# A recommendation tower on one core: the upper layers run one step behind their operands

## The chip, the cores and the metric

The kernel runs on one core of a Trainium2 chip. What is measured is the device time of one execution in microseconds (us); a smaller number is better. The engines are TensorE (PE in the profile, PEld its weight loads), VectorE (DVE), ScalarE (ACT), GpSimd (POOL) and SyncE (SP). Each works through its own queue in order; semaphores order them against one another.

## What is computed

For 512 samples 26 rows of 64 numbers are gathered from embedding tables; each is projected to 128 numbers and normalised, 26 are mixed down to 32, normalised again, and together with a normalised dense row they give 33 vectors per sample. Their pairwise products go through a linear layer with a norm and then through three dense layers.

```
x = layer_norm(dense_t @ Wd.T, gd, bd)
y = layer_norm(jnp.einsum('bnd,ed->bne', sparse_t, Ws), gs, bs)
y = jnp.einsum('bne,pn->bep', y, Wsi)
y = layer_norm(y, gsi, bsi)
T = jnp.concatenate([x[:, None, :], jnp.swapaxes(y, 1, 2)], axis=1)
Z = jnp.einsum('bnd,bmd->bnm', T, T)
Zflat = Z[:, TRIL_I, TRIL_J]
out = layer_norm(Zflat @ Wl.T, gl, bl)[:, :384]
h = jnp.concatenate([out, r_dense_t], axis=1)
h = jnp.maximum(h @ W_top1 + b_top1, 0.0)
h = jnp.maximum(h @ W_top2 + b_top2, 0.0)
y = h @ W_top3
```

All of it is in float32, so each matmul stands in the profile as two passes (x6 is three matmuls).

## The kernel before

**Blocks, units, steps.** The 512 samples are four blocks (0 to 3, `LAST` is 3) of 128, each block four units of 32 samples, 16 units in all (`NU`). Units 0, 4, 8 and 12 have four pairs of gathered rows, the others three. One loop of steps n = 0 to 16 is written out on every engine, as a software pipeline: step n takes unit n through `transposes` (L311), the copy `rowsT` (ACT L557), `gram` (L318) and the variance of its rows (DVE L744 to L750); it takes unit n-1 through `mix` (L334), `vsb` (ACT L569), `embed` (L344), `biased` (DVE L768), `squares` (ACT L574), the sums `tss` (DVE L774), `deviations` (ACT L579) and `normalised` (DVE L781, L783, which writes T); and unit n-2 through `interact` (L357) and `interactions` (ACT L586, L588), which leaves the pairwise products in `zs`. Here "step n" begins, on TensorE, when it transposes unit n.

**Through DRAM and back.** SP writes each unit's `zs` to a scratch in DRAM (L269, L271), waits until that has landed and reads it back in the layout that the linear layer wants: `products` (three transfers into `zr`, L235) and `singles` (one into `zr4`, L241, two into `z9`, L244). For each block it does so twice, for units 0 to 2 of the block and then for unit 3. The first of these also waits until the linear layer of the block before is through (`u_done`), since `zr`, `zr4` and `z9` exist once. In the last block ACT issues the last unit's `singles`.

**Upper layers.** `upper` is the linear layer of a block in six matmuls of 128x512 (parts 0 to 3 from `zr`, 4 from `zr4`, 5 from `z9`). Then come `upper_norm` and `upper_scaled` (ACT), `turn` (L384), `hidden1_dense` and `hidden1` (L400, L414, L408), `hidden2` (L426) and `answer` (L434). For blocks 0 and 1 they stand in the step loop at fixed lags behind the block's first unit: upper [0, 1, 2] at U0, [3, 4, 5] at U1, turn and hidden1 at MLP, hidden2 at TOP, answer at ANS. In a step they stand behind `interact`. Nearly all of these share one PSUM bank, `pU`, and so `upper(k)` waits until ACT has copied the answer of block k-1 out (`o_sb`, L637); for block 0 the bank is that of the setup's small products. `x_row` (ACT L601) writes one row of `z9` per block.

**Setup inside the loop.** The linear layer's weights are made while the first units run: `weight_sums` and `weight_means`, `centred_weights` (ACT L649), `s_rows` (PE L454, DVE L807 to L810), `single_rows` (PE L461, L462, DVE L819, L820), `centred_rows` (ACT L655 to L659), `hidden_weights` (DVE L825) and `hidden_bias` (PE L470, DVE L830).

**Gathers.** POOL issues the 104 indirect DMAs of all units, two for each pair; every unit has its own place in SBUF, so POOL waits for nobody.

Of the kernel before, what the change touches and what calls it, by code (L numbers as in the profile page):

```python
# [21 lines left out]
NL = 5  # L22
# [36 lines left out]
def build(nc, tables, index, consts, small, ws_t, gs_row, wsi_rows, dense_t, wd_t, wl, wlx, w1, w2, out):  # L59
# [3 lines left out]
    with ExitStack() as ctx:  # L63
# [144 lines left out]
        block = ctx.enter_context(nc.Block())  # L208

        LAST = NBLK - 1  # L210
        U0, U1, MLP, TOP, ANS = UNITS + 2, UNITS + 3, UNITS + 4, UNITS + 5, UNITS + 6
        READS = 12

        def unit_rows(n):
# [10 lines left out]
        def tile_T(n):  # L225

            k, m = divmod(n, UNITS)
            return T[:, k % 2, :, US * m:US * (m + 1), :]

        def products(queue, k, units):  # L230

# [14 lines left out]
        @block.sync  # L246
        def _(sp):
            for dst, src, done in [(idx_in[:], index, ld_index), (ws_sb[:], ws_t, ld_ws), (const[:], consts, ld_const),
                                   (wsi_sb[:], wsi_rows, ld_wsi), (gs_sb[:], gs_row, ld_gs), (cols[:], small, ld_cols),
                                   (wd_sb[:], wd_t, ld_wd), (dense_sb[:], dense_t, ld_dense), (wlx_sb[:], wlx, ld_wlx)]:  # L250
                sp.dma_start(dst, src).then_inc(done, 16)
            for j in range(NL):
                if j % 2 == 0:

                    sp.wait_ge(r_done, 1 + j // 2)
                sp.dma_start(wl_sb[:, j, :], wl[:, j, :]).then_inc(ld_wl[j], 16)
            for c in range((USED + DENSE) // P):
                if c % 3 == 0:
                    sp.wait_ge(r_done, 4 + c // 3)
                first = P * c if P * c < USED else P * c + UO - USED  # L260
                sp.dma_start(w1_sb[:, c, :], w1[first:first + P, :]).then_inc(ld_w1, 16)
            sp.dma_start(w2_sb[:], w2.rearrange("(c p) n -> p c n", p=P)).then_inc(ld_w2, 16)
            for n in range(NU):
                k, m = divmod(n, UNITS)
                if m == 0 and k >= 2:

                    sp.wait_ge(zr_sb, 16 * READS * (k - 1))
                sp.wait_ge(zs_sb, n + 1)
                sp.dma_start(zscr[k % 2, :, m].rearrange("r p f -> p r f"),  # L269
                             zs[:, n % 2, 0:4 * QG * G8].rearrange("p (r f) -> p r f", r=4)).then_inc(zw[n % 2], 16)  # L270
                sp.dma_start(zscr9[k % 2, m], zs[:, n % 2, 4 * QG * G8:]).then_inc(zw[n % 2], 16)  # L271
                if m == UNITS - 2:
                    sp.wait_ge(zw[n % 2], 32 * (n // 2 + 1))
                    sp.wait_ge(zw[(n - 1) % 2], 32 * ((n - 1) // 2 + 1))
                    if k:
                        sp.wait_ge(u_done, k)
                    products(sp, k, range(0, UNITS - 1))
                    singles(sp, k, range(0, UNITS - 1))
                if m == UNITS - 1:
                    sp.wait_ge(zw[n % 2], 32 * (n // 2 + 1))  # L280
                    products(sp, k, range(m, UNITS))
                    if k < LAST:
                        singles(sp, k, range(m, UNITS))
            sp.wait_ge(o_sb, NBLK)
            sp.dma_start(out, ysb[:]).then_inc(out_done, 16)
            sp.wait_ge(out_done, 16)
# [14 lines left out]
        def _(pe):  # L301
# [59 lines left out]
            def upper(k, part):  # L361

                if part[0] == 0:
# [2 lines left out]
                    pe.wait_ge(zr_sb, 16 * READS * (k + 1))  # L366
                    pe.wait_ge(xrow_sb, k + 1)
                    if k == 0:
                        pe.wait_ge(w_ready, NL)
                        pe.wait_ge(w9c_ready, 1)  # L370
                for j in part:
# [118 lines left out]
            for n in range(NU + 1):  # L490
# [8 lines left out]
                if n == 0:  # L499
                    x_turned()  # L500
                if n == NU:
                    upper(LAST - 1, [4])
                if n:
                    embed(n - 1)
                if n == 0:
# [8 lines left out]
                    s_rows(range(0, 3))  # L514
                if n == 4:
                    s_rows(range(3, NL))
                    single_rows()
                if n == 5:
                    hidden_bias()
                if (k := block_at(n, TOP)) is not None:  # L520
                    hidden2(k)
# [4 lines left out]
                if (k := block_at(n, MLP)) is not None:  # L526
                    hidden1_dense(k)
                    hidden1(k)
                if n == NU - 2:
                    upper(LAST - 1, [0, 1, 2])  # L530
                if n == NU - 1:
                    upper(LAST - 1, [3])
                if n == NU:
                    upper(LAST - 1, [5])
            interact(NU - 1)
            hidden1_dense(LAST - 1)
            turn(LAST - 1)
# [11 lines left out]
        def _(act):  # L549
# [118 lines left out]
            for n in range(NU + 1):  # L668
# [29 lines left out]
                    interactions(n - 2)  # L698
                if n in (1, 2, 3):
                    weight_sums(range(2 * n - 2, min(2 * n, NL)))  # L700
                if n in (4, 5):
                    centred_weights(range(3 * n - 12, min(3 * n - 9, NL)))
                if n == 5:
                    centred_rows()
                if (k := block_at(n, U0)) is not None:
                    x_row(k)
                if n == NU - 2:
                    x_row(LAST - 1)
# [7 lines left out]
            x_row(LAST)  # L716
            upper_turned(LAST - 1)
            act.wait_ge(zw[(NU - 1) % 2], 32 * ((NU - 1) // 2 + 1))
            singles(act, LAST, range(UNITS - 1, UNITS))
            relu1(LAST - 1)  # L720
            upper_norm(LAST)
            upper_scaled(LAST)
# [8 lines left out]
        def _(dve):  # L731
# [147 lines left out]
            for n in range(NU + 1):  # L879
# [8 lines left out]
                if n:  # L888
                    variances(n - 1)
                    normalised(n - 1)  # L890
                if n == 3:
                    weight_means()
                if n == 4:
                    s_rows()
                    single_rows()
                if n == 5:
                    hidden_weights()
                    hidden_bias()
            upper_inverse(LAST - 1)
# [68 lines left out]
```

## Time and profile before

| | us |
|---|---|
| time, median of 3 runs | 204.39 (202.47 to 205.0) |
| the profiled execution, its own time | 204.47 |
| its span in the trace | 202.7 |
| TensorE busy | 155.0 (76%) |
| VectorE busy | 116.8 (58%) |
| ScalarE busy | 85.2 (42%) |
| GpSimd busy | 102.9 (51%) |
| mean granted TensorE clock | 0.899 of full |

Busy times are sums over the span. Times in the rows below are counted from the span's start. A row of the timeline gives start, duration, engine, line, operation, tiles, count, and in brackets how long the engine was idle before it and what ended that.

### The profile page before, as it was taken

How to read it: one execution, taken by the hardware profiler on the slowest of the kernel's cores; microseconds unless marked ns; L12 is line 12 of the kernel's file. 1: busy time of each engine (PE TensorE's matmuls, PEld its weight loads, DVE VectorE, ACT ScalarE, POOL GpSimd, SP SyncE). 2: the span in 40 equal slices, each digit the busy share in tenths (PEclk: the TensorE clock that was granted, in tenths of full speed). 3: DMA queues.
4: the chain of work that ended last, by engine and by line, in shares of the span. 5: the costliest groups of instructions: out<-in, count | busy, mean ns of one | idle time of the engine just before them, and what ended most of it. 6: DMA issues, size and time to landing. Idle time of an engine off the chain costs nothing.

```text
span 202.7 us, 4648 instructions
## 1 busy us (share of the span) xinstructions
PE 155.0 (76%) x1865; PEld 106.3 (52%) x1865; DVE 116.8 (58%) x279; ACT 85.2 (42%) x229; POOL 102.9 (51%) x108
## 2 busy tenths in 40 slices
PE   0547787597806995599699939987995999496996
PEld 0435354463302683266497725657883464395684
DVE  2896239876828259819754990779099358600000
ACT  2002317735351193527526650546476034712063
POOL 3787777777777777777787777771000000000000
PEclk9995569889985699799999997999999699889999
DMA  5514132151935122312135241121411101152000
GB/s 143 173 27 129 32 124 81 25 186 37 269 67 76 28 58 37 57 26 55 28 73 65 52 69 26 29 55 44 53 32 18 31 0 31 32 63 36 0 3 0
DMA packets 38521, 12.01 MB, mean 59 GB/s; under 512 B 34114, under 2 KB 35266, under 8 KB 38499
## 3 DMA queue, kind: packets, MB, share of 16 engines
q1 hardware_dynamic: 34354, 8.26, 18.8%
q0 software_dynamic: 3328, 3.41, 8.3%
q8 instruction: 15, 0.25, 0.5%
q10 hardware_dynamic: 816, 0.02, 0.2%
q14 instruction: 8, 0.06, 0.1%
HBM read 9.46 MB, written 2.23 MB: 58 GB/s over the span
## 4 chain that ended last, share of the span: by engine, by line
PE 35%; POOL 16%; DMA 12%; DVE 11%; issue 9%; ACT 8%; SPq 7%; ACTq 0%; DVEq 0%
POOL rows L295 16%; PE pU L373 7%; DMA zscr<-zs 7%; PE pV L334 6%; PE pA L318 4%; SPq L235 3%; PE pU L414 3%; DVE t L768 2%; DVE evar L747 2%; DVE prod L744 2%; PE pU L400 2%; PE pA L373 2%; DMA z<-zscr 2%; PE pA L311 2%; ACT t L574 2%
## 5 line engine op out<-in xcount | busy, mean ns | idle before, releaser
L295 POOL DMA_INDIRECT rows<-in_tables,idx x104 | 102.7, 988 | 34.3 <-issue 31.4
L744 DVE TENSOR_TENSOR prod<-pA,rows 128x384 f32<-128x384 f32 (+1 forms) x16 | 9.4, 590 | 42.7 <-PE pA L318 42.6
L373 PE MATMUL pU<-wg,zr 128*128 128x512 f32 x24 | 17.4, 865 | 9.6 <-DMA z<-zscr 6.1
L334 PE MATMUL pV<-wexp,srow 128*64 128x192 f32 (+4 forms) x256 | 23.6, 335 | 0.7 <-DVE srow L759 0.7
L783 DVE TENSOR_TENSOR T<-t,trs 128x512 f32<-128x512 f32 x32 | 22.2, 694 | 1.1
L574 ACT ACTIVATE t<-t 128x512 f32<-128x512 f32 x32 | 19.5, 629 | 5.8 <-DVE t L768 5.7
L334 PEld LDWEIGHTS pV<-wexp,srow 128*64 128x64 f32 x256 | 17.7, 156 | 6.5 <-issue 2.7
L557 ACT COPY rowsT<-pA 128x384 f32<-128x384 f32 (+1 forms) x16 | 7.9, 497 | 31.0 <-PE pA L311 30.9
L318 PE MATMUL pA<-gbd,rowsT 128*128 128x128 f32 x104 | 18.7, 327 | 2.9 <-ACT rowsT L557 2.7
L768 DVE TENSOR_TENSOR t<-pT,bias 128x512 f32<-128x512 f32 x32 | 20.5, 683 | 0.4 <-PE pT L344 0.4
L774 DVE TENSOR_REDUCE tss<-t 128x16 f32<-128x512 f32 x32 | 20.4, 677 | 0.1
L357 PEld LDWEIGHTS pZ<-T 128*32 128x32 f32 x1024 | 11.9, 112 | 12.8 <-issue 6.4
L318 PEld LDWEIGHTS pA<-gbd,rowsT 128*128 128x128 f32 x104 | 15.4, 224 | 6.1 <-ACT rowsT L557 4.5
L344 PE MATMUL pT<-vsb,wscg 64*128 64x512 f32 x64 | 18.3, 648 | 0.0
L357 PE MATMUL pZ<-T 128*32 128x34 f32 x1024 | 14.1, 202 | 2.9 <-DVE T L783 2.9
L311 PE MATMUL pA<-const,rows 128*128 128x128 f32 x52 | 9.8, 307 | 8.3 <-DMA rows<-in_tables,idx 8.3
L311 PEld LDWEIGHTS pA<-const,rows 128*128 128x128 f32 x52 | 6.9, 158 | 16.4 <-issue 13.7
L373 PEld LDWEIGHTS pU<-wg,zr 128*128 128x128 f32 x24 | 7.2, 324 | 15.5 <-issue 15.3
L563 ACT ACTIVATE esd<-evar,eps 128x6 f32<-128x6 f32 (+1 forms) x16 | 4.8, 299 | 23.0 <-DVE evar L750 16.8
L569 ACT COPY vsb<-pV 128x512 f32<-128x512 f32 x16 | 9.3, 584 | 8.8 <-PE pV L334 8.5
L781 DVE RECIPROCAL trs<-tsd 128x16 f32<-128x16 f32 x32 | 7.9, 246 | 7.0 <-ACT tsd L579 6.9
L579 ACT ACTIVATE tsd<-tss,eps 128x16 f32<-128x16 f32 x32 | 9.4, 305 | 3.9 <-DVE tss L774 3.6
(153 smaller groups left out, 203.2 us busy)
## 6 DMA issues: line engine op xcount, KB each, us to landing
zscr<-zs SPq DMA_DIRECT2D x16, 128.0 KB, 2.0
rows<-in_tables,idx POOLq DMA_INDIRECT x104, 2.5
wl_sb<-in_wl SPq DMA_DIRECT2D x5, 256.0 KB, 2.7
w_sb<-in_w SPq DMA_DIRECT2D x5, 256.0 KB
dense_sb<-in_dense_t SPq DMA_DIRECT2D x1, 512.0 KB, 4.6
w_sb<-in_w SPq DMA_DIRECT2D x1, 512.0 KB, 6.3
zr<-zscr SPq DMA_DIRECT2D x4, 96.0 KB
zr<-zscr SPq DMA_DIRECT2D x4, 72.0 KB
```

The lines of the kernel that those rows point to most:

```text
L295: pool.indirect_dma_start(out=rows[:, j, h * D:(h + 1) * D], out_offset=None, in_=tables, in_offset=bass.IndirectOffsetOnAxis(ap=idx[:, 2 ...
L311: got = nc.tensor.transpose(pA[n % 2][:, P * j:P * (j + 1)], rows[:, first + j, :], ident)
L318: got = mm(pA[n % 2][:, P * j:P * (j + 1)], rowsT[:, n % 2, j, :], gbd[:], start=True, stop=True)
L334: got = mm(pV[(n - m + u) % 2][D * h:D * (h + 1), PJ * (a - US * u):PJ * (z + 1 - US * u)], srow[:, n % 2, i, D * h:D * (h + 1)], wexp[:, ...
L344: mm(pT[h][:], wscg[D * h:D * (h + 1), :], vsb[D * h:D * (h + 1), n % 2, :], start=True, stop=True).then_inc(y_done, 1)
L357: got = mm(pZ[PJ * s:PJ * (s + 1), NCOL * g:NCOL * (g + 1)], t[:, h, i, 0:PJ], t[:, h, i, :], start=True, stop=True)
L373: mm(upper_bank(k)[:], zr[:].rearrange("p a (g j) -> p (a g) j", j=4)[:, :, j], wg[:, j, :], start=j == 0, stop=False)
L574: a.activation(t2[:, h], t1[:, n % 2, h], ACT.Square).then_inc(t_sq, 1)
L744: v.tensor_tensor(prod[:, 0:count, :], pA[n % 2][:, 0:P * count].rearrange("p (j r) -> p j r", r=P), rows[:, first:first + count, :], ALU. ...
L768: v.tensor_tensor(t1[:, n % 2, h], pT[h][:].rearrange("p (a b) -> p a b", b=PJ), bias[:].unsqueeze(1).to_broadcast([P, US, PJ]), ALU.add). ...
L774: v.tensor_reduce(out=tss[:, h], in_=t2[:, h], op=ALU.add, axis=AX.X).then_inc(t_var, 1)
L783: v.tensor_tensor(tile_T(n)[:, h, :, 0:PJ], t1[:, n % 2, h], trs[:, h].unsqueeze(2).to_broadcast([P, US, PJ]), ALU.mult).then_inc(t_sb, 1)
```

## The change

- The lags U0, U1, MLP, TOP and ANS grow by one step each; `x_row` of blocks 0 and 1 stays in the step it was in.
- In the setup `single_rows` moves from step 4 to 5 and `hidden_bias` with `hidden_weights` from 5 to 6; on ACT `centred_weights` moves from steps 4 and 5 to 5 and 6 and `centred_rows` from 5 to 6; on DVE `weight_means` moves from step 3 to 4. `upper(0)` gets a wait for `b1_ready`.
- The linear layer of block 2 stood as [0, 1, 2] in step 14, [3] in step 15, [4] and [5] in step 16. It now stands as [0, 1] in step 15, and [2] and [3, 4, 5] in step 16.
- In block 3 the products are read back for units 0 and 1 and then for 2 and 3 (before: 0 to 2 and then 3).

```diff
-        U0, U1, MLP, TOP, ANS = UNITS + 2, UNITS + 3, UNITS + 4, UNITS + 5, UNITS + 6
+        U0, U1, MLP, TOP, ANS = UNITS + 3, UNITS + 4, UNITS + 5, UNITS + 6, UNITS + 7
...
+        def ahead(k):
+
+            return UNITS - 2 if k == LAST else UNITS - 1
...
-                if m == UNITS - 2:
+                if m == ahead(k) - 1:
                     sp.wait_ge(zw[n % 2], 32 * (n // 2 + 1))
                     sp.wait_ge(zw[(n - 1) % 2], 32 * ((n - 1) // 2 + 1))
                     if k:
                         sp.wait_ge(u_done, k)
-                    products(sp, k, range(0, UNITS - 1))
-                    singles(sp, k, range(0, UNITS - 1))
+                    products(sp, k, range(0, m + 1))
+                    singles(sp, k, range(0, m + 1))
                 if m == UNITS - 1:
                     sp.wait_ge(zw[n % 2], 32 * (n // 2 + 1))
-                    products(sp, k, range(m, UNITS))
+                    sp.wait_ge(zw[(n - 1) % 2], 32 * ((n - 1) // 2 + 1))
+                    products(sp, k, range(ahead(k), UNITS))
...
                     if k == 0:
+                        pe.wait_ge(b1_ready, 1)
...
                 if n == NU:
-                    upper(LAST - 1, [4])
+                    upper(LAST - 1, [2])
...
                 if n == 4:
                     s_rows(range(3, NL))
+                if n == 5:
                     single_rows()
-                if n == 5:
+                if n == 6:
                     hidden_bias()
...
-                if n == NU - 2:
-                    upper(LAST - 1, [0, 1, 2])
                 if n == NU - 1:
-                    upper(LAST - 1, [3])
+                    upper(LAST - 1, [0, 1])
                 if n == NU:
-                    upper(LAST - 1, [5])
+                    upper(LAST - 1, [3, 4, 5])
...
-                if n in (4, 5):
-                    centred_weights(range(3 * n - 12, min(3 * n - 9, NL)))
-                if n == 5:
+                if n in (5, 6):
+                    centred_weights(range(3 * n - 15, min(3 * n - 12, NL)))
+                if n == 6:
                     centred_rows()
-                if (k := block_at(n, U0)) is not None:
+                if (k := block_at(n, U0 - 1)) is not None:
                     x_row(k)
...
             act.wait_ge(zw[(NU - 1) % 2], 32 * ((NU - 1) // 2 + 1))
-            singles(act, LAST, range(UNITS - 1, UNITS))
+            act.wait_ge(zw[NU % 2], 32 * ((NU - 2) // 2 + 1))
+            singles(act, LAST, range(ahead(LAST), UNITS))
...
-                if n == 3:
+                if n == 4:
                     weight_means()
-                if n == 4:
                     s_rows()
+                if n == 5:
                     single_rows()
-                if n == 5:
+                if n == 6:
                     hidden_weights()
                     hidden_bias()
```

On TensorE, from the end of step 4, the order before was (L454 is `s_rows`, L461 and L462 `single_rows`, L311 the transposes that open step 5):

```order
L357 MATMUL pZ<-T 32x34 x32
L454 MATMUL pU<-wl_sb,beye 32x512 x2
L461 MATMUL pU<-wlx_sb,cols 1x512
L462 MATMUL pU<-wbraw,bp 1x512
L311 MATMUL pA<-const,rows 128x128 x3
L334 MATMUL pV<-wexp,srow 64x160 x2
```

In the changed kernel (its line numbers are up to six higher: L316 the transposes, L323 `gram`, L349 `embed`, L467 and L468 `single_rows`) the same place reads:

```order
L460 MATMUL pU<-wl_sb,beye 32x512 x2
L316 MATMUL pA<-const,rows 128x128 x3
L339 MATMUL pV<-wexp,srow 64x160 x2
L339 MATMUL pV<-wexp,srow 64x192 x4
L339 MATMUL pV<-wexp,srow 64x64 x2
L339 MATMUL pV<-wexp,srow 64x128 x2
L323 MATMUL pA<-gbd,rowsT 128x128 x3
L349 MATMUL pT<-vsb,wscg 128x512 x2
L362 MATMUL pZ<-T 32x34 x32
L467 MATMUL pU<-wlx_sb,cols 1x512
L468 MATMUL pU<-wbraw,bp 1x512
```

The single-row products now stand behind the whole of step 5's pipeline work.

On TensorE at the end, before, from the last part of step 14 on (L373, L376, L378 are the parts of `upper(2)`, the last row is `interact(15)`; the second L334 is `mix(15)`):

```order
L373 MATMUL pU<-wg,zr 128x512
L334 MATMUL pV<-wexp,srow 64x192 x4
L334 MATMUL pV<-wexp,srow 64x160 x2
L376 MATMUL pU<-wg,zr 128x512
L344 MATMUL pT<-vsb,wscg 128x512 x2
L357 MATMUL pZ<-T 32x34 x32
L378 MATMUL pU<-w9c,z 128x512
L357 MATMUL pZ<-T 32x34 x32
L400 MATMUL pT<-dense_sb,w_sb 128x128 x8
```

And in the changed kernel, from the end of step 15 on (L379, L382, L384 are the same parts):

```order
L379 MATMUL pU<-wg,zr 128x512 x2
L339 MATMUL pV<-wexp,srow 64x192 x4
L339 MATMUL pV<-wexp,srow 64x160 x2
L379 MATMUL pU<-wg,zr 128x512
L349 MATMUL pT<-vsb,wscg 128x512 x2
L362 MATMUL pZ<-T 32x34 x32
L379 MATMUL pU<-wg,zr 128x512
L382 MATMUL pU<-wg,zr 128x512
L384 MATMUL pU<-w9c,z 128x512
L362 MATMUL pZ<-T 32x34 x32
L406 MATMUL pT<-dense_sb,w_sb 128x128 x8
```

Three parts instead of one stand between the last two `interact`, and three instead of five ahead of the last `embed`.

On SP's queue the end of the loop was, before (each pair of L269 and L271 writes one unit; the first pair here is unit 14's):

```order
L269 DMA zscr<-zs 128x4x64
L271 DMA zscr<-zs 128x16
L235 DMA zr<-zscr 64x12x32
L235 DMA zr<-zscr 48x12x32
L235 DMA zr<-zscr 16x12x32
L241 DMA zr<-zscr 128x12x8
L244 DMA z<-zscr 32x12x8 x2
L269 DMA zscr<-zs 128x4x64
L271 DMA zscr<-zs 128x16
L235 DMA zr<-zscr 64x4x32
```

And now (from behind unit 13's write on):

```order
L239 DMA zr<-zscr 64x8x32
L239 DMA zr<-zscr 48x8x32
L239 DMA zr<-zscr 16x8x32
L245 DMA zr<-zscr 128x8x8
L248 DMA z<-zscr 32x8x8 x2
L273 DMA zscr<-zs 128x4x64
L275 DMA zscr<-zs 128x16
L273 DMA zscr<-zs 128x4x64
L275 DMA zscr<-zs 128x16
L239 DMA zr<-zscr 64x8x32
```

The writes of units 14 and 15 both stand behind the first read of the block, and so behind its wait for `u_done`.

## Rows read from the trace of the kernel before

**Rows 1.** The page: the chain that ended last, shares of the span by engine
```profile
PE 35%; POOL 16%; DMA 12%; DVE 11%; issue 9%; ACT 8%; SPq 7%; ACTq 0%; DVEq 0%
```
**Rows 2.** The waits: who waited for whom, us in total, times, longest
```profile
PE pU L373 <- DMA z<-zscr: 6.1, 2, 3.3
```
**Rows 3.** The gathers' line: ns min/median/max, first and last start, and their landing
```profile
L295 POOL DMA_INDIRECT rows<-in_tables,idx x104: 940/945/1575, 3.3 to 136.5; - x104
...
DMA to landing us min/median/max: 2.3/2.5/5.4
```
**Rows 4.** The timeline where steps 4 and 5 meet
```profile
57.05 0.32 ACT L586 COPY zs<-pZ 128x192 f32<-128x192 f32 x1 [2.27 <-DMA zscr<-zs]
...
57.38 2.23 ACT L649 ACTIVATE wg<-wl_sb,gg 128x512 f32<-128x512 f32 x3
...
59.51 0.49 ACT L579 ACTIVATE tsd<-tss,eps 128x16 f32<-128x16 f32 x2
...
62.57 1.01 PE L461 MATMUL pU<-wlx_sb,cols 32*1 32x512 f32 x1 [7.81 <-DVE wbraw L807]
...
63.21 0.47 DVE L810 TENSOR_SCALAR w<-wlx_sb,cols 32x512 f32<-32x512 f32 x1
```
**Rows 5.** The timeline of steps 5 to 8: DVE, ACT and PE
```profile
69.54 0.56 DVE L744 TENSOR_TENSOR prod<-pA,rows 128x384 f32<-128x384 f32 x1 [3.66 <-PE pA L318]
...
72.66 0.30 ACT L586 COPY zs<-pZ 128x192 f32<-128x192 f32 x1
...
76.00 0.49 ACT L579 ACTIVATE tsd<-tss,eps 128x16 f32<-128x16 f32 x2
...
78.14 1.27 DVE L825 TENSOR_SCALAR w1g<-w_sb,cols 128x512 f32<-128x512 f32 x3
...
83.42 4.42 PE L373 MATMUL pU<-wg,zr 128*128 128x512 f32 x6 [3.57 <-ACT z L601]
...
94.66 0.60 PE L311 MATMUL pA<-const,rows 128*128 128x128 f32 x4
```
**Rows 6.** The timeline of steps 10 to 14: PE, and ACT's copy of an answer
```profile
112.70 0.49 PE L311 MATMUL pA<-const,rows 128*128 128x128 f32 x3
...
118.34 0.24 ACT L637 COPY ysb<-pU 1x128 f32<-1x128 f32 x1
...
120.64 4.59 PE L373 MATMUL pU<-wg,zr 128*128 128x512 f32 x6 [3.28 <-DMA z<-zscr]
...
132.22 0.60 PE L311 MATMUL pA<-const,rows 128*128 128x128 f32 x4
...
143.69 0.49 PE L311 MATMUL pA<-const,rows 128*128 128x128 f32 x3
...
150.02 0.49 PE L311 MATMUL pA<-const,rows 128*128 128x128 f32 x3
```
**Rows 7.** Windows: stretch, its us, busy of each engine, PEclk, DMA share, GB/s
```profile
120.60:125.10 4.50, 4.46 (x7) 2.02 (x8) 0.98 (x3) 0.00 (x0) 3.41 (x4) 0.62 0.28 54
125.10:132.20 7.10, 7.10 (x100) 4.47 (x99) 4.49 (x10) 3.46 (x9) 5.45 (x6) 1.00 0.13 30
```
**Rows 8.** The timeline of the end: PE and SP's queue
```profile
167.85 1.14 PE L334 MATMUL pV<-wexp,srow 128*64 128x192 f32 x12 [0.40 <-DVE srow L759]
...
169.98 1.13 PE L344 MATMUL pT<-vsb,wscg 64*128 64x512 f32 x4
...
175.73 1.13 PE L357 MATMUL pZ<-T 128*32 128x34 f32 x64 [2.87 <-DVE T L783]
...
176.83 2.40 SPq L235 DMA_DIRECT2D zr<-zscr  x3
...
181.54 0.50 SPq L271 DMA_DIRECT2D zscr<-zs  x1
...
183.44 1.72 SPq L235 DMA_DIRECT2D zr<-zscr  x3
...
186.60 3.82 PE L373 MATMUL pA<-wg,zr 128*128 128x512 f32 x8 [2.01 <-DMA zr<-zscr]
```

More of the change, by code:

```diff
@@ L276, in _ @@
                         sp.wait_ge(u_done, k)
-                    products(sp, k, range(0, UNITS - 1))
-                    singles(sp, k, range(0, UNITS - 1))
+                    products(sp, k, range(0, m + 1))
+                    singles(sp, k, range(0, m + 1))
                 if m == UNITS - 1:
                     sp.wait_ge(zw[n % 2], 32 * (n // 2 + 1))
-                    products(sp, k, range(m, UNITS))
+                    sp.wait_ge(zw[(n - 1) % 2], 32 * ((n - 1) // 2 + 1))
+                    products(sp, k, range(ahead(k), UNITS))
                     if k < LAST:
-                        singles(sp, k, range(m, UNITS))
+                        singles(sp, k, range(ahead(k), UNITS))
             sp.wait_ge(o_sb, NBLK)
```

## The prediction, made before the changed kernel had run

> **What bounds the kernel now.** I read the chain of work that ended last first. TensorE has 35% of it, GpSimd only 16%, and DMA, DVE and "issue" share a third [rows 1]: no engine alone is the bound, so the question is where TensorE stands still. Then the gathers, since they feed everything: POOL issues its 104 from buffers of their own; the first starts at 3.3 us, the last at 136.5 [rows 3], one per 133.2 / 103 = 1.29 us, and the last lands at about 139. But step 15, which needs it, starts only at about 162: step 14 starts at 150.02 and is like step 10, which lasts from 112.70 to 125.1, 12.4 with its waits [rows 6, 7]. The gathers are 23 us ahead by then: from step 5 on the kernel is held by TensorE and what TensorE waits for. The timeline shows four long waits there: 7.81 us at 62.57 for the DVE copy of `s_rows` [rows 4], 3.57 us ahead of `upper(0)` for ACT's `x_row` [rows 5], 3.28 us ahead of `upper(1)` [rows 6] and the other wait for the same transfer ahead of `upper(2)`, 6.1 - 3.3 = 2.8 us [rows 2]. After the last three TensorE also runs slow: the window with `upper(1)` has a granted clock of 0.62, most of it at 1.2 GHz, the next one 1.00 [rows 7]. Three parts take 4.5 us there, where in the tail four take 3.82 us [rows 8], so 2.75 us for three is the price at full clock, 1.7 us less each time.
>
> **What holds the setup.** ACT gets `zs` of unit 2 off its hands only at 57.05, after waiting for unit 0's scratch write; then three `wg` (2.23 us) stand ahead of `tsd` at 59.51, which DVE needs for T and then for `s_rows`, through at 63.21 + 0.47 = 63.7 [rows 4]. TensorE sits at `single_rows` behind that.
>
> **The change, step by step.** I walk the start of each step, in the trace's own time. Steps 0 to 4 don't change, nor does the write that lands at 57.
>
> *Steps 5 to 7.* `zs` ends at 57.6 and `tsd` follows at once, 1.9 us earlier, so DVE is through `s_rows` at 61.8. The gathers of unit 5 (40 of them, 3.3 + 39 x 1.29 and 2.5 to land, so about 56.2) let TensorE start step 5 at once instead of waiting for `single_rows`; its `gram` waits for ACT's `rowsT` until 58.7 and is done well before 61.8. So `prod` of unit 5 starts at 61.8, now 69.54 [rows 5]. From here DVE and ACT hold the loop, by distances of rows 5 and 4. `prod` to `zs`: 72.66 - 69.54 = 3.1, so 64.9. `zs` to `tsd` with three `wg`: 59.51 - 57.05 = 2.5, so 67.4. `tsd` to the end of T: 78.14 - 76.00, 2.2 with its pipelining, so 69.6; then the two one-row copies of `single_rows`, 1.4 for two DVE instructions of 512 (estimated from `prod`, 0.56 for 384), so `prod` of unit 6 at 71.0. Step 6 again: `zs` 74.1; `tsd` behind two `wg`, `centred_rows` (76.00 - 72.66 = 3.3) and now `x_row` (0.3) at 77.75; T through at 79.95; `w1g` 1.27 and `b1p` 0.15: 81.4. Here is what the change gives back: setup work that TensorE no longer waits for still stands ahead of `rowsT` and T on ACT and DVE. `gram(7)` can start at 78.7; with `embed` and `interact` (one each at 0.9, 1.0, 0.7) TensorE reaches `upper(0)` at 81.5, where the new wait for `b1_ready` ends too, and [0, 1, 2] takes 2.75. **Step 8 starts at 84.3 at full clock.** TensorE will have stood 2 us or more ahead of `gram(7)`; with the slow clock that followed the waits of 3.57 and 3.28 us it would be up to 1.7 later. I take 85.0. Now it is 94.66, with parts [3, 4, 5] done, which cost 2.6.
>
> The Trainium skill, TensorE: Matmul & The Clock Gate, section "What's actually happening", says that the throttled state is the default and activity releases it; the window rows agree (0.62, then 1.00). By it the long wait that is left, ahead of `gram(7)`, would be followed by slow matmuls and step 8 would start near 86; by the full clock at 84.3.
>
> *Steps 8 to 15.* Each kind of step has a row at full clock. A step with [3, 4, 5]: 7.1 [rows 7], with a fourth pair 0.35 more, 7.45. A step with turn and hidden1: 143.69 - 132.22 = 11.5, its waits of some 1.8 for ACT in it. A step with hidden2: 150.02 - 143.69 = 6.3 [rows 6]. The step with [0, 1, 2] was 12.4 (112.70 to 125.1, the next step's start). There the transfer is a step old now, but the answer of the block before is copied out in the same step as before, and that is what is late next: ACT's copy ends at 118.34 + 0.24, so 5.9 us after the step's start [rows 6]. `upper` starts at 5.95 instead of 7.95, waits 1.3 instead of 3.3 and keeps its clock: 5.95 + 2.75 = 8.7. `mix` of these steps needs `srow` from DVE, whose loop is about 6.2 long, under each of them. Starts: step 9 at 92.45, 10 at 103.95, 11 at 110.25, 12 at 118.95, 13 at 126.4, 14 at 137.9, 15 at 144.2. In step 15 only two parts: 5.95 + 1.85, so `mix(15)` at **152.0**, now 167.85. The gathers stay ahead, by about 3 us at steps 9, 12 and 13 (their last lands at 115.7 for step 12) and 5 at step 15.
>
> *The end.* From `mix(15)` to `embed(15)` stands one part as before, 169.98 - 167.85 = 2.1: 154.1. From there to `interact(15)` is a chain over DVE and ACT, 175.73 - 169.98 = 5.75, with 2.87 of waiting in it [rows 8]; the two parts more that stand there now (1.7) fit into it. So 159.85. The linear layer of block 2 is through at 154.1 + 1.8 + 2.75 = 158.7. SP then issues six reads, 4.15 us (176.83 until the first of unit 15's two writes, 0.5 ahead of 181.54), until 162.9; then two writes of each of two units at 0.5, the last issued at 164.4, landed 1.9 later (183.44 - 181.54) at 166.3; then the last products, as before 186.60 - 183.44 = 3.15 after that: `upper(3)` at **169.45**, 9.6 after `interact(15)`, now 10.9. Behind 186.60 nothing changes: 202.7 - 186.6 = 16.1. Span 185.55, and 1.8 around it (204.47 - 202.7): 187.3; the profiled execution stands at the median, so that needs no correction. Sum by places: 5.7 in the setup with its slow clock, 7.4 in blocks 1 and 2 (two waits cut by 2.0 and 1.5, two slow stretches of 1.7, the rest rounding), 1.8 from two parts moved behind the last `embed`, 1.3 in the last read-back; 17 us with rounding.
>
> The new waits, bounded: `b1_ready` costs nothing to 1 us, as DVE and TensorE arrive together. SP's wait for `u_done` now holds the writes of units 14 and 15. Their cover is the chain to `interact(15)`: `zs` of unit 15 comes 1.7 after 159.85, at 161.6, and SP is free for it at 163.9 (now the data come 1.7 after 175.73, at 177.4, and the write is issued at 181.0). If `u_done` came 1 us later, the end would.
>
> **Rivals.**
> *A, forecast, 184 to 191.5:* above. Chance 0.74, and 0.02 for still less.
> *B, the setup keeps more.* ACT's and DVE's serial work in steps 5 to 7 is the only stretch for which no row shows the new order. If each of three loops costs 1.5 to 2.5 us more than the distances taken (a slow TensorE, a late landing: gathers took up to 5.4 [rows 3]), step 8 starts at 90 to 92: 192 to 199. Against it: DVE and ACT distances don't depend on TensorE's clock. 0.15.
> *C, waits come back elsewhere.* The step with [0, 1, 2] keeps its 12.4 and the slow clock, because some operand is still late: 3.7 us in each of two blocks, and B on top: 200 to 208. Against it: both transfers are issued a whole step before. 0.06.
> *D, slower: the gathers stretch.* In the changed kernel DVE works the same hours in fewer. If a gather waited while DVE runs, its pace would rise. It begins to cost when the pace passes 1.32 us (steps 9, 12, 13) and the kernel is slower by 2% when the last gather lands at 166, a pace of 1.55. For: the longest gather is 1575 ns. Against: median 945 and minimum 940 under a DVE that is busy 58% of the time [rows 3]. 0.03; a small stretch of 0.05 us only moves A to about 190.
> The Trainium skill, SBUF - State Buffer, names this mechanism: an exclusive lock on a port pair that VectorE shares with GpSimd, through which descriptors are written ("the DVE blocks DMA trap"). By that rule D would be likely; the trace does not show it, since the gathers' median lies 5 ns above their minimum.
>
> **The numbers.** Predicted 187.3. From 184 (full clock everywhere, 1 us less in the last read-back, early step 8) to 196 (most of B). A measurement here tells a difference of about 2%, 4 us. Faster takes A, B and the rare faster case: 0.91; the same C: 0.06; slower D: 0.03.
>
> **What would show it.** The wait at `single_rows` is gone; the first `prod` after it starts near 62; the longest TensorE wait is the one ahead of `gram(7)`; `upper(1)` and `upper(2)` start about 6 us into their steps with a granted clock of 1.00; between the last two `interact` TensorE waits under 2 us; the last read-back is issued within 7 us of `interact(15)`. Wrong would be: step 8 later than 88, a wait of 3 us ahead of `upper(1)`, transposes that wait for gathers after step 6 by more than a us, gathers at more than 1.35 us.

## The result

The changed kernel takes 193.58 us in the median (192.1 to 195.37), the kernel before in the same session 204.69 (202.47 to 206.72); the ratio is 0.947, with a 95% interval of 0.934 to 0.960. Timed twice more it gave 192.31 and 192.33 us, at ratios of 0.948 and 0.944. So the change makes the kernel 5.2 to 5.6% faster, some 11 us. Forecast were 187.3 us, or 17 us, with a range of 184 to 196. Executions of one kernel spread by 1 to 4%, and one of the kernel with ACT's order changed took 240.97 us at a mean granted clock of 0.603; medians given here are of all executions, ratios of the faster ones alone.

The profiled execution took 192.1 us, with a span of 190.3. First the page: busy times hardly moved (155.0 to 153.4 us on TensorE, 116.8 to 117.2 on DVE), and the chain that ended last now has more of TensorE and of the gathers in it, and less than half of the DMA (5% instead of 12%) [rows 1].

```profile
PE 153.4 (81%) x1865; PEld 106.1 (56%) x1865; DVE 117.2 (62%) x279; ACT 84.4 (44%) x229; POOL 103.1 (54%) x108
...
PE 40%; POOL 20%; DVE 12%; issue 10%; ACT 7%; DMA 5%; SPq 4%; ACTq 0%
```

The place where steps 4 and 5 meet, in the timeline of the changed kernel (start, duration, engine, line, and in brackets the idle time and its end), which answers to [rows 4]:

```profile
56.77 0.32 ACT L591 COPY zs<-pZ 128x192 f32<-128x192 f32 x1 [1.76 <-DMA zscr<-zs]
...
57.10 0.52 ACT L584 ACTIVATE tsd<-tss,eps 128x16 f32<-128x16 f32 x2
...
57.82 0.70 PE L316 MATMUL pA<-const,rows 128*128 128x128 f32 x3 [2.66 <-DMA rows<-in_tables,idx]
...
60.90 0.48 DVE L816 TENSOR_SCALAR w<-wlx_sb,cols 32x512 f32<-32x512 f32 x1
...
62.22 0.56 DVE L750 TENSOR_TENSOR prod<-pA,rows 128x384 f32<-128x384 f32 x1 [0.84 <-PE pA L323]
...
64.00 0.59 PE L467 MATMUL pU<-wlx_sb,cols 32*1 32x512 f32 x1
```

TensorE no longer stands 7.81 us at the single rows: it reaches them at 64.00 without a wait and has done step 5 ahead of them. `tsd` follows `zs` at once, `s_rows` are through at 61.4 (63.7 before), and `prod` of unit 5 starts at 62.22 instead of 69.54.

Steps 6 to 8, which answer to [rows 5]:

```profile
68.69 0.94 PE L323 MATMUL pA<-gbd,rowsT 128*128 128x128 f32 x6 [1.98 <-ACT rowsT L562]
...
71.62 2.81 PE L476 MATMUL pU<-cols,w_sb 128*128 128x1 f32 x24
...
74.79 1.95 PE L339 MATMUL pV<-wexp,srow 128*64 128x192 f32 x16
...
79.33 1.65 PE L323 MATMUL pA<-gbd,rowsT 128*128 128x128 f32 x6 [2.59 <-ACT rowsT L562]
...
80.91 2.08 PE L349 MATMUL pT<-vsb,wscg 64*128 64x512 f32 x4
...
84.03 3.48 PE L379 MATMUL pU<-wg,zr 128*128 128x512 f32 x6
...
87.34 0.60 PE L316 MATMUL pA<-const,rows 128*128 128x128 f32 x4
```

Here are the waits that took over: two for ACT's `rowsT`, 1.98 and 2.59 us. Around the second lies a slow stretch (`gram` 1.65 us, 0.94 at full clock). It doesn't begin with the wait: `mix(6)`, ahead of it, takes 1.95 us already, where `mix(5)` took 1.20, and the window that ends as `gram(7)` starts has a granted clock of 0.58:

```profile
74.30:79.30 5.00, 2.44 (x21) 1.79 (x20) 2.15 (x5) 4.89 (x14) 4.07 (x4) 0.58 0.29 57
```

(columns: us, busy of PE, PEld, DVE, ACT, POOL, granted clock, DMA share, GB/s). By windows of 1 us the clock is 1.00 until 75 and 0.50 from 76 to 85. What stands ahead of its fall is `hidden_bias` (L476), 24 passes of one column each. Step 8 starts at 87.34, 94.66 before.

Blocks 1 and 2, which answer to [rows 6]:

```profile
112.35 0.49 PE L316 MATMUL pA<-const,rows 128*128 128x128 f32 x3
...
118.28 2.96 PE L379 MATMUL pU<-wg,zr 128*128 128x512 f32 x6 [1.04 <-ACT ysb L642]
...
128.38 0.49 PE L316 MATMUL pA<-const,rows 128*128 128x128 f32 x3
...
139.61 0.49 PE L316 MATMUL pA<-const,rows 128*128 128x128 f32 x3
...
145.67 0.49 PE L316 MATMUL pA<-const,rows 128*128 128x128 f32 x3
```

`upper(1)` comes 5.9 us into its step, waits 1.04 us for the copy of the answer instead of 3.28 for the transfer, and its three parts take 2.8 us instead of 4.4, with a granted clock of 1.00.

And the end, which answers to [rows 8]: TensorE first, then SP's queue.

```profile
156.00 1.13 PE L349 MATMUL pT<-vsb,wscg 64*128 64x512 f32 x4
...
161.74 0.77 PE L362 MATMUL pZ<-T 128*32 128x34 f32 x64 [1.03 <-DVE T L789]
...
172.52 5.52 PE L379 MATMUL pA<-wg,zr 128*128 128x512 f32 x8 [3.23 <-DMA zr<-zscr]
```
```profile
163.09 2.08 SPq L248 DMA_DIRECT2D z<-zscr  x2
...
166.74 0.51 SPq L275 DMA_DIRECT2D zscr<-zs  x1
...
168.50 1.76 SPq L239 DMA_DIRECT2D zr<-zscr  x3
```

`interact(15)` starts at 161.74, 14.0 us earlier than before. But from there to the end of the span it is 28.6 us, before 202.7 - 175.73 = 27.0. The end got longer by 1.6 us where 1.3 less was forecast: the wait ahead of `upper(3)` grew from 2.01 to 3.23 us, and its first four parts from 3.7 to 5.4 us to the next part's start. From `interact(15)` to `upper(3)` it is 10.8 us, as good as before (10.9); the wait is longer because TensorE has its own work ahead of it done in 7.5 us instead of 8.9. Before, that work had begun at the lower clock, behind the 2.87 us ahead of `interact(15)` (`hidden1_dense` 3.00 us, now 2.05).

### The profile page after: what moved, and what is told of

It is laid out like the page before. It is cut to its first block, busy times and chain, and to the rows that moved or that the text cites. A ratio compares the mean times of both kernels' runs of the same rounds, so it can differ in the third digit from the quotient of the medians.

```text
span 190.3 us, 4653 instructions
## 1 busy us (share of the span) xinstructions
PE 153.4 (81%) x1865; PEld 106.1 (56%) x1865; DVE 117.2 (62%) x279; ACT 84.4 (44%) x229; POOL 103.1 (54%) x108
## 3 DMA queue, kind: packets, MB, share of 16 engines
q0 software_dynamic: 3328, 3.41, 10.8%
## 4 chain that ended last, share of the span: by engine, by line
PE 40%; POOL 20%; DVE 12%; issue 10%; ACT 7%; DMA 5%; SPq 4%; ACTq 0%
POOL rows L300 20%; PE pU L379 6%; PE pV L339 6%; PE pA L323 5%; PE pT L349 3%; PE pA L379 3%; PE pU L420 3%; PE pZ L362 2%; DVE t L774 2%; PE pU L406 2%; DVE evar L753 2%; DVE prod L750 2%; DMA rows<-in_tables,idx 2%; PE pA L316 2%; SPq L239 2%
## 5 line engine op out<-in xcount | busy, mean ns | idle before, releaser
L339 PE MATMUL pV<-wexp,srow 128*64 128x192 f32 (+4 forms) x256 | 24.3, 343 | 0.2 <-DVE srow L765 0.2
L323 PE MATMUL pA<-gbd,rowsT 128*128 128x128 f32 x104 | 18.6, 326 | 6.6 <-ACT rowsT L562 6.4
L339 PEld LDWEIGHTS pV<-wexp,srow 128*64 128x64 f32 x256 | 18.2, 160 | 6.3 <-issue 3.1
L323 PEld LDWEIGHTS pA<-gbd,rowsT 128*128 128x128 f32 x104 | 15.3, 222 | 9.7 <-ACT rowsT L562 7.9
L349 PE MATMUL pT<-vsb,wscg 64*128 64x512 f32 x64 | 19.8, 699 | 0.0
L362 PEld LDWEIGHTS pZ<-T 128*32 128x32 f32 x1024 | 12.2, 112 | 12.4 <-issue 8.5
L316 PE MATMUL pA<-const,rows 128*128 128x128 f32 x52 | 9.5, 300 | 10.1 <-DMA rows<-in_tables,idx 10.1
L316 PEld LDWEIGHTS pA<-const,rows 128*128 128x128 f32 x52 | 6.4, 152 | 17.5 <-issue 15.0
L362 PE MATMUL pZ<-T 128*32 128x34 f32 x1024 | 14.6, 203 | 1.1 <-DVE T L789 1.0
L379 PE MATMUL pU<-wg,zr 128*128 128x512 f32 x24 | 13.5, 681 | 2.3 <-ACT ysb L642 2.3
L794 DVE RECIPROCAL urs<-usd 128x1 f32<-128x1 f32 x4 | 0.8, 192 | 19.0 <-ACT usd L612 18.9
```

The costliest lines, as they stand in the source:

```text
L316: got = nc.tensor.transpose(pA[n % 2][:, P * j:P * (j + 1)], rows[:, first + j, :], ident)
L323: got = mm(pA[n % 2][:, P * j:P * (j + 1)], rowsT[:, n % 2, j, :], gbd[:], start=True, stop=True)
L339: got = mm(pV[(n - m + u) % 2][D * h:D * (h + 1), PJ * (a - US * u):PJ * (z + 1 - US * u)], srow[:, n % 2, i, D * h:D * (h + 1)], wexp[:, ...
L349: mm(pT[h][:], wscg[D * h:D * (h + 1), :], vsb[D * h:D * (h + 1), n % 2, :], start=True, stop=True).then_inc(y_done, 1)
L362: got = mm(pZ[PJ * s:PJ * (s + 1), NCOL * g:NCOL * (g + 1)], t[:, h, i, 0:PJ], t[:, h, i, :], start=True, stop=True)
L379: mm(upper_bank(k)[:], zr[:].rearrange("p a (g j) -> p (a g) j", j=4)[:, :, j], wg[:, j, :], start=j == 0, stop=False)
```

## The experiments

Each kernel was timed against the kernel before on the same chip, in three sessions. The changed kernel itself was timed in the first (with the kernels up to "The setup undone") and in the third (with the matmuls in step 7), but not in the second. For the four kernels of the second session the difference to the changed kernel is given both between medians and between ratios to the kernel before, and neither is sure to 1 us.

**The changed kernel again.**

> The changed kernel again, beside its variants. Expected 192 to 194 us, with the two things that the prediction undersized: steps 6 to 8 slow (step 8 at about 87) and a wait of about 3 us ahead of upper(3), after which it runs slow.

192.31 us, ratio 0.948 (0.937 to 0.958). Its trace differs from the first in one place that matters. The windows from 79.0 to 84.6 us of the first trace and of this one:

```profile
79.00:84.60 5.60, 5.27 (x75) 3.44 (x76) 5.43 (x14) 1.85 (x5) 4.21 (x5) 0.50 0.14 24
```
```profile
79.00:84.60 5.60, 5.47 (x80) 3.73 (x81) 5.46 (x14) 1.90 (x5) 4.08 (x6) 0.96 0.12 23
```

From `gram(7)` on, the first trace runs at 1.2 GHz (0.50) into `upper(0)`, the second nearly all at 2.4. In the second TensorE had been slow earlier, in most of step 6 (66 to 72) and again in the first part of step 7 (76 to 79), where DVE and ACT cover it, and so it waited only 0.27 us ahead of `gram(7)`. It reached `upper(0)` at 81.90, just as `b1p` was there (81.52 + 0.15), and step 8 started at **84.67**: the forecast's 84.3 at full clock. In the first, `b1p` was there at 81.87 and `upper(0)` started at 84.03 all the same. `gram(7)` starts within 0.2 us of the same time in both (79.33 and 79.13), and from there to step 8 it is 8.0 us in the first and 5.5 in the second. So the same kernel has 2.7 us of play at step 8, by where the slow stretch falls. At the end both traces show the same: a wait of 3.23 and 3.61 us ahead of `upper(3)`, which takes 5.52 us.

**The last block's split undone.**

> The changed kernel with the last block read back as before (units 0 to 2, then 3). Theory S, the split carries a part of the gain (my sum gave the read-back 1.3 us): slower than the changed kernel by 1.3 us or more. Theory N, the smaller last read gives back what the earlier write gains: unit 14's data at 159.6, landed at 163, six reads of 4.15, unit 15's writes landed at 169.6, upper(3) at 172.7 against 172.5: same within 0.5 us, and still a wait of some 3 us ahead of upper(3).

```diff
         def ahead(k):
 
-            return UNITS - 2 if k == LAST else UNITS - 1
+            return UNITS - 1
```

192.25 us against 192.31: same. Theory N holds. TensorE and SP's queue at the end of this kernel:

```profile
159.75 0.77 PE L362 MATMUL pZ<-T 128*32 128x34 f32 x64 [1.03 <-DVE T L789]
...
170.83 2.04 PE L379 MATMUL pA<-wg,zr 128*128 128x512 f32 x3 [3.54 <-DMA zr<-zscr]
```
```profile
160.64 2.39 SPq L239 DMA_DIRECT2D zr<-zscr  x3
...
165.34 0.50 SPq L275 DMA_DIRECT2D zscr<-zs  x1
...
167.32 1.72 SPq L239 DMA_DIRECT2D zr<-zscr  x3
```

`upper(3)` comes 11.1 us after `interact(15)`; in the changed kernel 10.8 in the first trace and 170.57 - 159.41 = 11.2 in the second. The reads of units 0 to 2 start at 160.64 here, of units 0 and 1 at 160.80 in the changed kernel: both stand just behind the end of `upper(2)`, and SP's time for six reads follows. The smaller last read is quicker (170.83 - 167.32 = 3.5 us from its issue to `upper(3)`, against 172.52 - 168.50 = 4.0), the later write eats that up. This part of the change is worth nothing that can be measured here.

**The setup alone.**

> The kernel before with the setup moved one step (single rows in 5, hidden bias, hidden weights and centred rows in 6) and the lags as they were. Theory C, the two halves need each other: the wait at the single rows goes, but upper(0) then stands in step 6 behind b1p, which DVE has at about 82: a wait of 7 us there, step 7 at about 86 instead of 87.8, 1 to 2 us gained in all (203). Theory I, the parts add up: 5 us or more gained (under 200).

```diff
                 if n == 4:
                     s_rows(range(3, NL))
+                if n == 5:
                     single_rows()
-                if n == 5:
+                if n == 6:
                     hidden_bias()
```

(with the same moves on ACT and DVE as in the change, and the wait for `b1_ready`). 204.62 us (202.67 to 207.18), where the kernel before had 206.48 over its wide spread of 202.11 to 209.71. The shortest executions of the two differ by 0.6 us, so no gain is shown; theory I, 5 us or more, is out. Its trace shows why:

```profile
81.92 4.31 PE L374 MATMUL pU<-wg,zr 128*128 128x512 f32 x6 [7.74 <-DVE b1p L832]
```

The 7.81 us that stood at the single rows stand in step 6 instead, 7.74 us for `b1p`, with the slow clock at their end still (4.31 us for three parts). Step 7 starts at 86.07, 87.68 before, which is theory C's 86. The wait has moved, as the setup's chain on DVE and ACT was not made shorter.

**The setup undone.**

> The changed kernel with the setup where it was before, so lags, block 2 in three pieces and the last block's split alone. The 7.8 us wait at the single rows stays, the waits ahead of upper(1) and upper(2) shrink to about 1.2 us at full clock. Theory C: step 8 at about 90 instead of 87.3, 3 us slower than the changed kernel (196), so this half carries three quarters of the gain. Theory I, the setup is worth its 7.8 us: slower than the changed kernel by 6 us or more (199).

```diff
                 if n == 4:
                     s_rows(range(3, NL))
+                    single_rows()
                 if n == 5:
-                    single_rows()
-                if n == 6:
                     hidden_bias()
```

(and likewise on ACT and DVE). 196.08 us, 3.8 slower than the changed kernel; ratio 0.964 (0.953 to 0.975). That is nearer to theory C (3 us) than to the 6 us or more of theory I. So the lags and the pieces of block 2 carry 3.6% by themselves, some two thirds of the gain; the setup adds 1.6% to them, and alone no gain is shown. The lags and the pieces of block 2 were not taken apart, so the 1.8 us that the forecast gave to the pieces were not tested. In the trace of this kernel the wait at the single rows is there (6.24 us) and the waits ahead of `upper(1)` and `upper(2)` are 1.25 and 1.28 us, near the changed kernel's 1.04 and 1.28. Step 8 starts at 92.35 there, not at about 90: ahead of it stand a wait of 2.57 us for DVE's `srow` and a slow `mix(6)` (2.18 us). That execution, 198.09 us, was the longest of the four.

**ACT's order in the setup.**

> The changed kernel with ACT's weight work taken out of the place ahead of tsd and rowsT: three wg in step 6 and two wg with the centred rows in step 7, behind vsb, where ACT stands idle 3.4 to 3.8 us. Theory A, ACT's order in steps 5 and 6 gives back the setup gain: the waits of 1.98 and 2.59 us ahead of gram(6) and gram(7) go, TensorE keeps its clock, step 8 starts at 82 to 83.5 (then held by its gathers) instead of 87.3, total 4 to 5 us less. Rival G, the gathers or DVE hold these steps: under 2 us less.

```diff
+                if n in (6, 7):
+                    centred_weights(range(3 * n - 18, min(3 * n - 15, NL)))
+                if n == 7:
+                    centred_rows()
                 if n < NU:
                     row_deviation(n)
...
-                if n in (5, 6):
-                    centred_weights(range(3 * n - 15, min(3 * n - 12, NL)))
-                if n == 6:
-                    centred_rows()
```

188.99 us, ratio 0.925 (0.913 to 0.937), against 0.948 and 0.944 for the changed kernel: 3.3 us less by medians, 3.8 to 4.6 by ratios. ACT and TensorE in its steps 6 to 8:

```profile
73.43 0.30 ACT L591 COPY zs<-pZ 128x192 f32<-128x192 f32 x1
...
74.28 0.31 ACT L584 ACTIVATE tsd<-tss,eps 128x16 f32<-128x16 f32 x1
...
74.99 0.46 ACT L562 COPY rowsT<-pA 128x384 f32<-128x384 f32 x1
...
75.50 1.65 PE L323 MATMUL pA<-gbd,rowsT 128*128 128x128 f32 x6 [0.50 <-ACT rowsT L562]
...
77.69 0.15 DVE L836 TENSOR_TENSOR b1p<-pU,cols 128x4 f32<-128x4 f32 x1
```
```profile
91.15 0.52 PE L316 MATMUL pA<-const,rows 128*128 128x128 f32 x3 [0.33 <-DMA rows<-in_tables,idx]
```

`tsd` comes 0.9 us after `zs` instead of 3.8 (74.62 to 78.41 in the changed kernel), the waits for `rowsT` fall to 0.70 and 0.50, and `b1p` is there at 77.7 instead of 81.9. Step 8 starts at 83.40. Theory A holds in its main part: ACT's serial weight work ahead of `tsd` and `rowsT` was what gave the setup gain back. One part of it fails. TensorE does not keep its clock: with only 0.50 us of waiting ahead of `gram(7)`, the granted clock is 0.50 from 75 to 81 all the same, and `gram(7)` takes 1.65 us, `embed` 2.08 and `upper(0)` 3.42. So the slow stretch of step 7 does not come from the wait ahead of `gram(7)`. The next limit shows too, transposes that wait for their gathers in steps 9, 12 and 13 (0.33, 0.40, 0.24 us).

**Matmuls in the wait ahead of `upper(3)`.**

> The changed kernel with three matmuls of 128x512 whose result nobody reads, put where TensorE waits 3.2 us ahead of upper(3). They take 2.6 us and fit. Theory W, the wait costs twice, by itself and by the lower clock behind it: upper(3) takes 3.7 instead of 5.4 us for its first four parts and the total falls by 1.5 to 1.7 us. Rival: upper(3) is slow for another reason (its operands just landed): no change.

```diff
             hidden1(LAST - 1)
+            for _ in range(3):
+                mm(pA[1][:], ident, w1_sb[:, 0, :], start=True, stop=True)
             upper(LAST, range(0, NL + 1))
```

190.83 us, ratio 0.935 (0.920 to 0.950), 1.5 us below the changed kernel by medians, 1.8 to 2.6 by ratios; intervals overlap, so the trace decides:

```profile
161.20 0.77 PE L362 MATMUL pZ<-T 128*32 128x34 f32 x64 [1.03 <-DVE T L791]
...
168.58 2.74 PE L546 MATMUL pA<-w_sb,const 128*128 128x512 f32 x6
171.41 3.82 PE L379 MATMUL pA<-wg,zr 128*128 128x512 f32 x8
```

With the wait filled, the same four parts take 3.82 us instead of 5.52, and from `interact(15)` to the end of the span it is 187.5 - 161.2 = 26.3 us instead of 28.6. The wait ahead of `upper(3)` cost twice: 1.7 us of its price is the lower clock behind it. The granted clock from 171.4 to 175.1 is 1.00, in the changed kernel it is 0.68 from 172.5 to 177.9; so the rival, that the operands had only just landed, is out. The kernel before says the same: there `upper(3)` starts as its operands land and takes 3.82 us too.

**The read-back buffers twice.**

> The changed kernel with zr, zr4 and z9 twice, so that the reads of a block wait for the linear layer two blocks back only. In block 3 SP then reads units 0 and 1 early and has the writes of units 14 and 15 out as soon as their data are there. Theory Q, SP's queue held by u_done sets the end: unit 15 landed at about 166 instead of 168.5, upper(3) at 169.3 to 170 and at full clock, total 4 to 5 us less. Rival: the landing time of the last read sets it: under 2 us less.

```diff
-        zr = sb("zr", [P, 4 * UNITS, G8 * 4])
+        zr = sb("zr", [P, 2, 4 * UNITS, G8 * 4])
...
-                    if k:
-                        sp.wait_ge(u_done, k)
+                    if k > 1:
+                        sp.wait_ge(u_done, k - 1)
```

(`zr4` and `z9` likewise, each use indexed by k % 2, and `x_row` waiting one block further back.) 187.53 us, ratio 0.913 (0.900 to 0.926): 6 to 7 us below the changed kernel by ratios, 4.8 by medians across sessions. SP's queue and TensorE:

```profile
154.50 1.76 SPq L239 DMA_DIRECT2D zr<-zscr  x3
...
163.75 1.33 SPq L275 DMA_DIRECT2D zscr<-zs  x1
...
166.17 1.76 SPq L239 DMA_DIRECT2D zr<-zscr  x3
```
```profile
170.20 2.11 PE L379 MATMUL pA<-wg,zr 128*128 128x512 f32 x4 [0.67 <-DMA zr<-zscr]
```

The reads of units 0 and 1 are issued at 154.5, while `mix(15)` runs, and the last unit's write no longer stands behind them: 8.2 us from `interact(15)` (161.99) to `upper(3)` instead of 10.8, and a wait of 0.67 us that leaves the clock alone. To the end of the span 24.3 us, 4.3 less. Theory Q holds. The gain by medians, 4.8 us, is about what the trace shows. The rest of the gain by ratios, 2 to 3 us, is not explained; it may be the spread of the kernel before (7.7 us in that session), but that is not shown.

**Both together.**

> Both: ACT's order and the second set of read-back buffers. If the two theories hold and don't share a cause, the gains add up to 8 to 10 us below the changed kernel, 183 to 185, unless the gathers bind (the last lands at 139 and step 15 would start at about 141).

184.36 us (183.86 to 185.01), ratio 0.904 (0.894 to 0.913): the fastest of the kernels here, 8 us below the changed one by medians (3.3 and 4.8 us were the two gains alone), so the two gains add up. Its span is 182.4. Nothing waits ahead of `gram(7)` any more, and still the granted clock is 0.50 from 72 to 78, from `hidden_bias` (3.56 us) on. Step 8 starts at 82.40, and steps 9 and 12 wait 0.43 and 0.61 us for gathers. Its gathers:

```profile
L300 POOL DMA_INDIRECT rows<-in_tables,idx x104: 940/944/1581, 3.4 to 136.9; - x104
```

The pace of the gathers is that of [rows 3], with DVE busy 64% of the span instead of 58%.

**Matmuls in the wait of step 7.**

> The changed kernel with three matmuls of 128x512 whose result nobody reads in step 7, behind mix, where TensorE waits 2.6 us for ACT's rowsT ahead of gram(7). Theory W, what made steps 7 and 8 later than forecast is the lower clock that follows this wait: gram(7) at 0.94 instead of 1.65 us, embed 1.1 instead of 2.1, upper(0) 2.9 instead of 3.5, step 8 starts at 84.3 to 85.5 instead of 87.3, and the time falls by up to 2 us. Rival V, DVE and ACT hold step 7 (b1p at 81.9) and the clock there is covered: step 8 no earlier than 86.5.

```diff
+                if n == 7:
+                    pe.wait_ge(t1_sb, 12)
+                    for _ in range(3):
+                        mm(pT[0][:], ident, w1_sb[:, 0, :], start=True, stop=True)
                 if n < NU:
                     gram(n)
```

> The changed kernel once more, on the same chip as the run with extra matmuls in step 7: 192 to 194 us; its trace shows how much steps 6 to 8 move from execution to execution (step 8 at 87.34 in the first trace, 84.67 in the second).

192.50 us, against 192.33 for the changed kernel in the same session (ratios 0.947 and 0.944): no gain. Theory W is not borne out: step 8 starts at 89.35, not at 84.3 to 85.5. In the trace with the extra matmuls TensorE ran at 1.2 GHz in `gram(6)` and `embed(6)` (71 to 75) and again from `hidden_bias` on (78 to 81), so that it came to the extra matmuls only at 81.35. ACT's `rowsT` was there at 81.50, so there was no wait left to fill, and the extra matmuls held `gram(7)` back until 84.03. It took 0.83 us and `upper(0)` 2.94, at full clock, but later than without them. A filler helps only where the wait is sure to be.

The third trace of the changed kernel, timed beside this one, has step 8 at 88.27, later than either of the first two. Its slow stretch, too, begins at 76, ahead of the wait of 2.63 us for `rowsT`. Taken together, ten traces have `hidden_bias` in this place. In nine of them the clock falls while it runs or within 1.3 us of its end, whatever wait follows (none to 7.7 us). In the tenth, that with matmuls ahead of `upper(3)`, it falls only behind the wait ahead of `gram(7)` (3.32 us). In the kernel before, `hidden_bias` stood behind a stretch that was slow until 69.7, and the clock stayed full behind it. No run moved or widened `hidden_bias`, so what makes the clock fall there is open.

## Why the prediction was right, and where not

**What bounds, right.** TensorE and what it waits for was the bound; behind step 6 the gathers hold a step only when ACT's order is changed too, and then by 0.61 us at most. The rival that the gathers stretch under a busier DVE (D) fell: 947 ns in the median in the changed kernel, 945 before, 944 in the kernel with both improvements. The Trainium skill, SBUF — State Buffer, section "Who interferes with whom", says that `tensor_tensor` has no two-port mode, and `tensor_reduce` none on this chip; it is in such a mode that VectorE blocks a transfer of GpSimd's. These two kinds are over four fifths of DVE's busy time here, so "by that rule D would be likely" was too strong, and the gathers' times agree with that.

**Steps 5 to 7, right in their chain.** Forecast and seen: `prod` of unit 5 at 61.8 and 62.22, of unit 6 at 71.0 and 71.50, `tsd` of step 6 at 77.75 and 78.41, `b1p` at 81.4 and 81.87. That the setup gives most of its gain back on ACT and DVE was in the forecast; the kernel with the setup alone and the one with ACT's order changed show it. Step 5 started at 57.82 instead of 56.2, since its gathers took 3.6 to 5.0 us to land and not 2.5; DVE waited 0.84 us for `gram(5)` by it.

**Step 8, mis-sized.** 85.0 was forecast, seen 87.34, and 84.67 in the second trace. The term is the slow clock from `gram(7)` on, for which I took 0.7 us of a bound of 1.7. From `gram(7)` to step 8 the first trace takes 2.5 us more than the second; `gram(7)` itself came 0.6 later than forecast. The bound was drawn too low: the slow stretch takes `gram` (+0.7), `embed` (+1.0), `interact` (+0.4) and part of `upper(0)` (+0.5), not `upper(0)` alone. And the reason given was not the right one: I had the stretch follow the wait ahead of `gram(7)`, but in the first trace it begins in `mix(6)`, before the wait, and with ACT's order changed it is there with next to no wait.

**Steps 8 to 15, right.** From step 8 to 15 the forecast has 59.2 us, seen were 58.3; each step from its row is off by 0.3 us at most. The wait for the answer's copy, named as what is late next, is there with 1.04 to 1.28 us.

**The end, wrong.** The step that failed is the one from `interact(15)` to the end. Forecast 25.7 us (9.6 and 16.1), seen 28.6 (10.8 and 17.8). Two terms of the sum are off. First, the read-back: SP's six reads took 4.4 us for the 4.15 taken, and the last read 4.0 for 3.15, since it holds two units now and I carried over the time of one; together 1.2 us with rounding. This takes away all but 0.1 of the 1.3 us that the sum by places gave to the last read-back, and the kernel with the split undone shows the same: it is worth nothing. Second, "behind 186.60 nothing changes" does not hold: the wait ahead of `upper(3)` came to 3.23 us, and `upper(3)` ran at a clock of 0.68, for 1.7 us more. I had priced the slow clock at three waits that went and not at the one that grew, though the same rows priced it. Before, the wait of 2.01 us left the clock alone; that TensorE comes to `upper(3)` earlier, by a shorter and full-clock stretch ahead, made the wait longer. Step 8 and the end, 2.3 and 2.9 us, less 0.5 for the steps between, make up the 4.7 us by which the profiled execution exceeds the forecast.

**The sum by places** of the forecast adds up to 16.2 us, and its walk gives 17.1. The walk is the one to go by: its starts give about 7 us in the setup (94.66 - 85.0 - 2.6), where the sum by places says 5.7.

**The signs.** Those that held: no wait at `single_rows`, `prod` near 62, `upper(1)` and `upper(2)` 6 us into their steps at full clock, 1.03 us between the last two `interact`, the last read-back issued 6.8 us behind `interact(15)`. One did not: the longest wait of TensorE behind step 5 is not the one ahead of `gram(7)` (2.59 us) but that ahead of `upper(3)` (3.23), the very one that was not priced. And step 8 later than 88 was to be a sign of being wrong: the first two traces have 87.34 and 84.67, the third 88.27.

**The rivals.** The forecast A named 184 to 191.5; the measured 193.58 lies above that, in the range of B (the setup keeps more, 192 to 199). B gave the right number for another reason: of the 4.7 us only 2.3 are in the setup, and step 8 is at 87.34, not at 90 to 92. B had named a slow TensorE as one of its causes, which is what most of the 2.3 us are, but in each of three loops; it shows in one. That the time still lies within the range of 184 to 196 owes as much to the width of the range as to the walk. C (the step with [0, 1, 2] keeps its 12.4 us) fell: that step took 8.7. A wait did grow at a place that C did not name, ahead of `upper(3)`, where SP's queue decides. I had looked at SP's new wait for `u_done` and called the writes covered, although my own figures had SP free only 2.3 us behind the data (163.9 and 161.6). It was 3.2 us in the trace (the first write of unit 15 issued at 166.25, its data there at 163.07), and the second set of buffers, with which the queue is free, gives 4.3 us.

## What to carry to other kernels

A wait on TensorE of over 3 us ahead of `upper(3)` cost 1.7 us more than itself: price the clock behind a wait that grows as well as behind one that goes. But look where the slow stretch begins before blaming a wait for it; in step 7 it began ahead of the wait, and the matmuls put there were no help. Moving a consumer back by a step removes its wait only if the chain that feeds it isn't moved along; ask what stands ahead of the last producer on its own in-order queue, and put setup work where that engine is idle. When a transfer is split anew, take the time of the piece that is now last from its own size.

## What the runs showed of the hardware

TensorE stood 2.01 us ahead of `upper(3)` in the kernel before and 2.38 with the setup alone, and the four parts behind took 3.82 us, at 2.4 GHz; it stood 3.23, 3.61 and 3.72 us in the changed kernel and with the setup undone, and they took 5.52, 5.52 and 6.28, partly at 1.2 GHz. With the wait filled they took 3.82 again. Not every slow stretch follows a wait: ahead of step 7's `gram` the clock fell in nine of ten traces during or just behind `hidden_bias`, 24 passes of one column on a busy TensorE, and not behind the 1.98 us ahead of `gram(6)`. Two executions of one kernel placed a slow stretch in different steps (0.50 and 0.96 in the same window), and this moved a step's start by 2.7 us.

The Trainium skill, TensorE: Matmul & The Clock Gate, section "HAM oscillation", tells of a DMA wait being followed by cold matmuls in each round of a loop. The wait ahead of `upper(3)` agrees with it, with 5.52 us behind the open wait of 3.23 us against 3.82 behind the filled one.

Gathers issued from GpSimd kept their pace (median 944 to 947 ns) while DVE's busy share of the span rose from 58 to 64%.
